# A recommendation tower's pairwise dot products: two half-width Gram matmuls per sample in place of one

## The reference

```python
sd = jnp.einsum('bfd,bd->bf', sparse_values, dense_features)
ss = jnp.einsum('bfd,bgd->bfg', sparse_values, sparse_values)
pairs = ss[:, iu, ju]                      # f < g
h = concat([dense, sd, pairs, dense], axis=1)          # 607 columns
h = jnp.maximum(h @ W_top1 + b_top1, 0.0)  # 512
h = jnp.maximum(h @ W_top2 + b_top2, 0.0)  # 256
y = h @ W_top3                             # 512 x 1
```

## Time and profile before

| | |
|---|---|
| three runs | 150.77, 148.31, 150.51 us; median 150.51 |
| the profiled execution's own time | 148.93 us |
| its span, first to last instruction | 147.1 us |
| mean granted TensorE clock | 0.826 |
| busy: TensorE matmuls, weight loads, VectorE, ScalarE, GpSimd | 95.5, 77.3, 74.3, 62.2, 67.5 us |
| Gram matmuls (L367) | 1024 passes, the first at 73.5, the last at 136.2 us |
| copies of `move_gram` | 72 on VectorE, 23.8 us; 72 on ScalarE, 23.9 us |
| gathers (L290) | 64, 66.8 us |

### The profile page before, as it was taken

The page is one execution under the profiler, slowest core; times in us unless marked ns, Lnnn a source line. Parts: engine busy times, 40 slices in busy tenths (PEclk is TensorE's granted clock), DMA queues, the critical chain, the costliest instruction groups (busy, mean ns, idle before and its releaser), DMA issues.

```text
span 147.1 us, 3329 instructions
## 1 busy us (share of the span) xinstructions
PE 95.5 (65%) x1420; PEld 77.3 (53%) x1420; DVE 74.3 (50%) x169; ACT 62.2 (42%) x130; POOL 67.5 (46%) x70
## 2 busy tenths in 40 slices
PE   0387999999799910000023395573997849989893
PEld 0255888888588810000012283342976738877781
DVE  1497999999966400000000079290728381476811
ACT  4323929667291440000111069090729273475500
POOL 3787887878778777777714507255000000000000
PEclk9999999999999995555555555555599999999999
DMA  3899949479932112212110201102000000000000
GB/s 60 259 395 359 288 104 304 137 160 401 357 98 56 54 54 52 54 48 50 46 40 18 54 7 40 36 22 54 4 0 4 4 0 0 4 4 0 4 0 3
DMA packets 6849, 13.37 MB, mean 91 GB/s; under 512 B 2353, under 2 KB 3506, under 8 KB 6834
## 3 DMA queue, kind: packets, MB, share of 16 engines
q1 hardware_dynamic: 4112, 8.95, 19.1%
q0 software_dynamic: 2048, 4.20, 10.0%
q10 hardware_dynamic: 674, 0.01, 0.3%
HBM read 13.15 MB, written 0.00 MB: 89 GB/s over the span
## 4 chain that ended last, share of the span: by engine, by line
PE 34%; issue 29%; POOL 15%; DVE 7%; ACT 6%; DMA 6%; DVEq 0%; another core or an unknown queue 0%; ACTq 0%
POOL rows L290 15%; PE gram L367 12%; DVE Z L562 5%; PE gram L338 5%; DMA rows<-in_tables_gather,idx 5%; PE hidden L395 5%; PE second L411 4%; ACT Z L487 4%; PE stage L321 3%; PE hidden L384 2%; PE second L409 2%; PE hidden L338 2%; ACT ET L478 1%; DMA idg<-in_ids_gather 1%; PE stage L395 1%
## 5 line engine op out<-in xcount | busy, mean ns | idle before, releaser
L290 POOL DMA_INDIRECT rows<-in_tables_gather,idx x64 | 66.8, 1044 | 33.2 <-issue 18.3
L562 DVE COPY Z<-gram 32x112 f32<-32x112 f32 (+3 forms) x72 | 23.8, 331 | 54.0 <-PE gram L367 53.1
L367 PE MATMUL gram<-ET 128*32 128x27 f32 x1024 | 19.0, 214 | 36.3 <-issue 35.2
L367 PEld LDWEIGHTS gram<-ET 128*32 128x32 f32 x1024 | 15.4, 130 | 41.7 <-issue 40.7
L487 ACT COPY Z<-gram 32x112 f32<-32x112 f32 (+3 forms) x72 | 23.9, 332 | 25.2 <-PE gram L367 24.5
L546 DVE TENSOR_SCALAR onehot<-ids,rowid 128x1024 fp32r<-128x1024 int16 (+1 forms) x48 | 28.6, 657 | 4.3 <-DMA ids<-in_ids_one 1.8
L338 PE MATMUL gram<-onehot,part 128*128 128x512 f32 x80 | 22.1, 428 | 6.5 <-DVE part L552 6.2
L338 PEld LDWEIGHTS gram<-onehot,part 128*128 128x128 f32 x80 | 16.1, 207 | 10.6 <-DVE onehot L546 7.2
L338 PE MATMUL hidden<-onehot,part 128*128 128x512 f32 x80 | 19.7, 397 | 1.0 <-issue 1.0
L338 PEld LDWEIGHTS hidden<-onehot,part 128*128 128x128 f32 x80 | 14.6, 188 | 4.1 <-issue 1.2
L552 DVE TENSOR_TENSOR part<-raw,part 128x1024 fp32r<-128x1024 f32 (+2 forms) x11 | 12.2, 1126 | 3.1 <-issue 2.0
(11 more groups left out here) (36 smaller groups left out, 42.5 us busy)
## 6 DMA issues: line engine op xcount, KB each, us to landing
raw<-in_tables_one SPq DMA_DIRECT2D x9, 512.0 KB, 3.1
ids<-in_ids_one SPq DMA_DIRECT2D x4, 256.0 KB
rows<-in_tables_gather,idx POOLq DMA_INDIRECT x64
W1s<-in_W_pairs SPq DMA_DIRECT2D x1, 768.0 KB
W1d<-in_W_dense SPq DMA_DIRECT2D x1, 512.0 KB
W2s<-in_W_top SPq DMA_DIRECT2D x1, 512.0 KB
raw<-in_tables_one SPq DMA_DIRECT2D x1, 384.0 KB
ids<-in_ids_one SPq DMA_DIRECT2D x2, 128.0 KB
```

The source lines that it names most:

```text
L290: pool.indirect_dma_start(out=rows[:, m % ROWS_RING, :], out_offset=None, in_=x["tables_gather"], in_offset=bass.IndirectOffsetOnAxis(ap=i ...
L367: last = pe.matmul(gram[p % 2][32 * i:32 * i + 32, NV * j:NV * (j + 1)], ET[:, VP * b:VP * (b + 1)], ETv[:, b, 0:NV], start=True, stop=True)
L562: last = dve.tensor_copy(dst, src)
```

## The change

A sample's Gram matrix is made by two matmuls, one that streams its even vectors 0, 2, ... 26 and one that streams its odd ones 1, 3, ... 27 (column 27 is one of the repeats), 14 columns each, with the same 32 columns as weights. They go into neighbouring quarters of the partitions: sample 2j to quarters 0 and 1, sample 2j+1 to quarters 2 and 3. A piece of 64 samples so has 128 matmuls in place of 64 (256 passes, and as many weight loads, in place of 128) and fills 448 columns of the bank in place of 432. A pair of quarters then goes to a pair of quarters of Z, so a piece has four moves of 64 partitions and 7 slots x 32 samples (7 x 16 in a piece of 32) in place of sixteen of 32 partitions and 7 or 6 slots x 16 (x 8): two on VectorE and two on ScalarE.

```diff
+EVERY = VP // 2 - 2
...
-        def z_moves(p, samples):
+        def z_moves(p, h):
...
-            for q in range(4):
-                ns = len(range(q, NV, 4))
-                for i in samples:
-                    src = gram[p % 2][32 * i:32 * i + 32, 0:size // 4 * NV].rearrange(
-                        "p (j c) -> p j c", c=NV)[:, :, q:q + 4 * (ns - 1) + 1:4]
-                    dst = Z[32 * q:32 * q + 32, t % ZT, 0:ns, b0:b0 + size].rearrange(
-                        "p s (j i) -> p j s i", i=4)[:, :, :, i]
-                    yield dst, src
+            for half in range(2):
+
+                src = gram[p % 2][64 * h:64 * h + 64, 0:size // 2 * EVERY].rearrange(
+                    "p (j s k) -> p j s k", s=SLOTS, k=2)[:, :, :, half]
+                dst = Z[64 * half:64 * half + 64, t % ZT, 0:SLOTS, b0:b0 + size].rearrange(
+                    "p s (j i) -> p j s i", i=2)[:, :, :, h]
+                yield dst, src
...
-                n = size // 4 // parts
+                n = size // 2 // parts
                 for j in range(n * k, n * (k + 1)):
                     for i in range(4):
-                        b = b0 + 4 * j + i
-                        last = pe.matmul(gram[p % 2][32 * i:32 * i + 32, NV * j:NV * (j + 1)], ET[:, VP * b:VP * (b + 1)],
-                                         ETv[:, b, 0:NV], start=True, stop=True)
+                        b = b0 + 2 * j + i // 2
+                        last = pe.matmul(gram[p % 2][32 * i:32 * i + 32, EVERY * j:EVERY * (j + 1)], ET[:, VP * b:VP * (b + 1)],
+                                         ETv[:, b, i % 2:i % 2 + 2 * EVERY - 1:2], start=True, stop=True)
...
-                for dst, src in z_moves(p, (2, 3)):
+                for dst, src in z_moves(p, 1):
...
-                for dst, src in z_moves(p, (0, 1)):
+                for dst, src in z_moves(p, 0):
```

## The result

The changed kernel takes 169.88 us (169.44 to 172.56), the kernel before 150.64 beside it: a ratio of 1.136, interval 1.116 to 1.156. Forecast were 153.7, at most 157.5. The direction was right, the size was not. The profiled execution took 169.75 us with a span of 167.9, 20.8 more than before. A kernel's time is given as the median of all its executions, but ratios leave out the slow ones, over 1.5% above the fastest of the same kernel, so a ratio can differ by a per cent from the quotient of two medians.

What follows compares the result with a forecast made beforehand. It took TensorE as the bound at the low clock and waits on moves, folds and `take_even` at the high one. The profiled 148.93 + 5.2 (low clock) - 0.4 (high clock) gave 153.7 us, range 148.5 to 157.5.

Steps and rivals of the forecast that it cites:

- The bound of before: Second half of the kernel: TensorE bounds pieces 0 to 3; waits for moves, fold and `take_even` bound pieces 4 to 8.
- the case in which all waits go: Rival, Gram matmuls: 14-column passes cost half, so Gram time stays and 5.3 us of waits go, 143.6 us; 6 in 100.
- The moves: VectorE and ScalarE: a new move takes 550 ns; a piece of 64 needs 1.8 us less, one of 32 1.4 less.
- The Gram matmuls: TensorE: doubled passes at unchanged spacing, set by weight loads, add 1.73 or 1.11 us per piece of 64, low or high clock.
- what I don't see: Whole kernel: unforeseen effects, such as fetching 2048 more instructions, a slower strided stream or moves gaining more; 8 in 100.
- The series rule: Rival, Gram passes: weight load and stream run one after the other, so half the stream is saved; 149.4 us, 15 in 100.
- The low clock: Pieces 0 to 3: 6.9 us of added passes, less 0.44, 0.4 and 0.85, so piece 4 starts 5.2 us later.
- The high clock: Piece 4 to the end: shorter moves pay for the doubled passes and little more, together -0.4 us.
- The early clock: Rival, pieces 1 to 3: unbroken work brings the high clock back early; 151.9 us, or 148.8 if it stays; 25 in 100.
- The stream alone: Rival, Gram passes: only streamed columns set a pass's price, so Gram time stays and waits go; 143.6 us, 6 in 100.
- The slow spells counting passes: Rival, pieces 2 and 3 beside the gathers: a set number of passes goes slowly, adding some 4 us each; 162 us, 4 in 100.

Runs made afterwards that it cites:

- the changed kernel's second run: The changed kernel, unchanged, run again on a chip where the kernel before takes about 150 us: 170.86 us, ratio 1.148.
- the recovery with one pass a matmul: The changed kernel with ET in bfloat16, so each matmul is one pass: 142.16 us beside 151.1 for the float32 kernel before.

## Why the prediction was wrong, step by step

**The bound of before.** Right where it names the waits: with the new moves alone they were down to 0.30 us in pieces 4 and 5. That this kernel is 5.3 us faster by the medians, exactly the sum that the prediction has for the case in which all waits go, is luck: 2.8 us of stops stand in it, and the interval of the ratio spans 1.1 to 4.4%.

**The moves.** Right: 532 ns on average over the long and the short form together, 550 forecast for the long one.

**The Gram matmuls.** Here it failed, at one sentence: "The number of passes and of weight loads doubles ... What sets a pass's time?" The price taken was that of an unbroken pass, and the sum then charged passes and nothing for the instructions that make them. 2048 more instructions stand in the prediction's last paragraph among "what I don't see", within 8 in 100. They were the larger term: 13.0 us of stops and some 3 of lower clock, against 4.8 in the sum. The kernel before could have warned: a piece's Gram matmuls were 256 instructions, one block, in a piece of 6.5 us, and the supply's 3.5 to 4 us a block lay beneath it unseen. The rows did not show a price, though, and the bound from both sides that they did allow (a block no faster than it ever came in the look-ups or in the pieces) was not drawn.

The spacing itself was right (13.1 and 8.4 ns for 13.5 and 8.7), but by luck: the reason for it, the weight load, was wrong. Half the weights leave it at 12.7 and 8.2 to 8.4 ns, 4 streamed columns at 13.0. A pass with its load has a price of its own here, whatever its columns. The Trainium skill, "TensorEngine Tiling (Array Packing)", Instruction Overhead, states a cost of some 60 cycles below which a short matmul doesn't fall. The round of four at the low clock, 51 to 54 ns or 61 to 65 cycles, agrees with it; at the high clock a round takes 33 to 35 ns, some 80 cycles, and there the rule is short by a quarter. The series rule weighed in the prediction gave 10.5 ns and falls.

**The low clock.** 8.4 us to piece 4 for 5.2; the missing part is, in the main, two stops of 3.35 us in piece 1. The rest of the sum comes out, from b8's transposes to layer 1 behind piece 3, at 3.46 - 0.84 = 2.6 more for 2.7 measured, but partly by luck: stops of 0.46 and 1.13 us and 0.46 us won by b9's transposes at the high clock are in the 2.7. The slow spells kept about their time (4.1 us in pieces 2 and 3, 4.6 and 4.8 before) and did not count passes.

**The high clock.** Forecast -0.4 (the terms add up to -0.45), measured +12.4: stops of 9.7 us and some 3 of the low clock. That the shorter moves would cover the doubled passes fits what is left, -0.3.

**The rivals.** The early clock did not come in piece 1 or 2. It came for 2.6 us at the start of piece 3 in this profile, and not in that of the changed kernel's second run; later the clock was lower than before, behind the stops. The stream alone and the series are refuted by the same spacings. The slow spells counting passes is refuted by their lengths. The range's upper end, 157.5, had no place for a cost that no row priced.

## What the instruction supply is, and what stays open

Blocks of 256 instructions of TensorE come no faster than one in 3.5 to 4.0 us, on three chips and in all forms of the Gram matmul that were tried; that is 14 to 16 ns an instruction, so by this estimate the limit binds wherever a load and a matmul together take less than some 28 ns, as the column-tiled passes with 8.4 to 13.5 ns do. Kernels with 1816, 2840, 3864 and 4888 matmuls and loads have 7, 11, 15 and 19 packets in the queue.

The time of a block has three parts, as in the example of piece 4 above. At the 128 stops of 0.35 us or more at such places, in sixteen of the profiles, the fetch took 0.88 to 1.50 us and TensorE went on 1.2 to 1.7 us after its end; the next fetch began 1.03 us after that at the soonest. The Trainium skill, "Runtime: NRT & Kernel Launch", Instruction fetch mechanics, gives the same block, 16 KiB or 256 instructions, and takes its fetch to be mostly hidden; the size agrees with the 19 packets for 0.31 MB and with the period of the stops, but here the fetch isn't hidden: 13.05 us of stops stand behind it.

Shown: the period, its constancy under half the weights and fewer streamed columns, the fetch that ends 1.2 to 1.7 us before TensorE goes on, the 14 ns for each added instruction, and the recovery with one pass a matmul. Not shown: what those 1.2 to 1.7 us are, what starts a fetch and why it isn't started sooner, and why the gathers slow TensorE on one chip and not on the two others.

## What to carry to other kernels

Count the instructions of a stretch as a resource with a price of its own: small column-tiled matmuls on TensorE get through 256 instructions in 1.2 to 2.0 us, and the next block is not there before 3.5. A change that halves the work of such small instructions and doubles their number gained nothing on the engine here and ran it dry, and the same copies are worth having only if they don't cost instructions elsewhere. In the timeline such a stop shows as "issue" ahead of an instruction that waits for nothing, with a constant number of instructions between two stops: count them, and look for a packet of the instruction queue just ahead.

## What was not expected of the hardware

- The instruction supply's limit, above: 14 ns an instruction in steady small matmuls.
- Four column-tiled passes in a round take 51 to 54 ns at the low clock whether they load 32 or 16 columns of weights (at 16: (1.79 - 0.18)/127 = 12.7 ns a pass, 51 a round) and whether they stream 27, 14 or 4 (13.5, 13.1 and 13.0 ns a pass).
- Gathers by GpSimd slow TensorE down to one to six small passes in 0.7 to 2.8 us on one chip, while programs with the same gathers on two others have no such spell: 150 against 115 us for one kernel.
- The clock fell behind the changed kernel's stops of 2.20 and 2.48 us in pieces 4 and 5 (0.67 and 0.80 in the stretches that follow) and stayed at 1.00 in the same pieces before, with waits of 1.73 and 2.16 us. Behind the stop of 2.17 us in piece 6 it stayed at 1.00 too, so the length of one pause alone doesn't tell.
